# Preparation of a GNN kernel as one block: degree gathers beside the edge rows, normalising on ScalarE, the node table stored inside

## The reference

```python
deg = segment_sum(ones_like(d), d, num_nodes)         # d: edge targets and self loops
dinv = where(deg > 0, rsqrt(deg), 0.0)
norm = dinv[s] * dinv[d]
h = layernorm(x) @ W1                                 # 256 -> 128
out = segment_sum(h[s] * norm[:, None], d) + b1
```

## Time and profile before

| | us |
|---|---|
| median of three runs | 4687.03 |
| profiled execution, its own time | 4687.02 |
| its span, first to last instruction | 4685.2 |
| PE busy | 2944.8 |
| DVE busy | 2124.8 |
| POOL busy | 2607.7 |
| ACT busy | 769.9 |
| preparation (to the first gather of the convolution) | 182.47 |
| its three parts end near | 71.4, 166, 182 |

### The profile page before, as it was taken

The page is one execution under the profiler, slowest core; times in us unless marked ns, Lnnn a source line. Parts: engine busy times, 40 slices in busy tenths (PEclk is TensorE's granted clock), DMA queues, the critical chain, the costliest instruction groups (busy, mean ns, idle before and its releaser), DMA issues. The chain is left out here.

```text
span 4685.2 us, 48041 instructions
## 1 busy us (share of the span) xinstructions
PE 2944.8 (63%) x13048; PEld 2229.0 (48%) x13048; DVE 2124.8 (45%) x3783; ACT 769.9 (16%) x1807; POOL 2607.7 (56%) x2735
## 2 busy tenths in 40 slices
PE   2444444444344444444538989967888777867998
PEld 1333333333233333333437744446666666646665
DVE  7522222222422222222645344447777777864344
ACT  1200000000000000000324422223333333314222
POOL 3577777777477777776350042137777777742000
PEclk9766555556655555566659999978888888875999
DMA  3422222222222222221323355444444444430000
GB/s 93 91 53 53 53 53 53 53 53 53 56 53 53 53 53 53 53 53 45 103 92 118 108 173 197 170 156 139 139 139 138 135 139 138 140 120 21 16 16 24
DMA packets 200949, 409.95 MB, mean 87 GB/s; under 512 B 51843, under 2 KB 125203, under 8 KB 193780
## 3 DMA queue, kind: packets, MB, share of 16 engines
q0 software_dynamic: 102144, 246.72, 19.4%
q1 hardware_dynamic: 91252, 156.35, 9.6%
q10 hardware_dynamic: 7296, 3.70, 0.6%
HBM read 305.82 MB, written 104.44 MB: 88 GB/s over the span
## 5 line engine op out<-in xcount | busy, mean ns | idle before, releaser
L654 POOL DMA_INDIRECT ring<-t_gcn,idx x1568 | 1492.0, 952 | 564.8 <-issue 477.3
L682 PE MATMUL psum<-ring,big 128*128 x3328 | 754.5, 418 | 1095.9 <-DMA ring<-t_gcn,idx 1095.9
L682 PEld LDWEIGHTS psum<-ring,big 128*128 128x128 f32 x3328 | 702.2, 321 | 1242.4 <-issue 1242.4
L1521 POOL DMA_INDIRECT xs_ring<-t_msg,idx x832 | 798.9, 960 | 380.4 <-issue 253.1
L703 DVE TENSOR_TENSOR big<-big,psum 128x1024 f32 x208 | 254.0, 1221 | 1523.0 <-PE psum L682 1522.3
L1644 PE MATMUL psum<-xs_ring,a_hot 128*128 128x264 f32 x1456 | 406.8, 439 | 0.0
L1644 PEld LDWEIGHTS psum<-xs_ring,a_hot 128*128 128x128 f32 x1456 | 330.1, 227 | 74.7
L847 ACT ACTIVATE m_xa<-big,dinv 128x128 f32<-128x128 f32 x49 | 19.5, 401 | 2066.4 <-PEq L641 2066.4
L1409 PE MATMUL psum<-big,a_xnt 128*128 128x512 f32 x784 | 355.2, 596 | 0.5 <-ACT a_xnt L1381 0.5
L1314 POOL DMA_INDIRECT a_back<-t_y,m_addr x98 | 98.0, 1000 | 438.8 <-POOLq L1118 279.8
L430 DVE TENSOR_TENSOR big<-dloc,psum 128x1024 f32<-128x1024 f32 x208 | 252.3, 1214 | 11.3 <-PEq L609 7.2
(11 more groups left out here) (402 smaller groups left out, 4254.0 us busy)
## 6 DMA issues: line engine op xcount, KB each, us to landing
t_msg<-a_rows SPq DMA_DIRECT2D x49, 1056.0 KB, 3.9
a_near<-t_near SPq DMA_DIRECT2D x52, 512.0 KB, 4.3
ring<-t_gcn,idx POOLq DMA_INDIRECT x1568, 2.5
m_xin<-t_tok SPq DMA_DIRECT2D x105, 128.0 KB, 2.1
t_y<-m_yb SPq DMA_DIRECT2D x105, 128.0 KB, 2.0
xs_ring<-t_msg,idx POOLq DMA_INDIRECT x832
xs_ring<-in_x SPq DMA_DIRECT2D x7, 896.0 KB, 11.2
t_gcn<-big SPq DMA_DIRECT2D x14, 448.0 KB, 3.3
```

Source lines behind the costliest of these rows:

```text
L654: g.indirect_dma_start(out=ring[:, p % HALF_RING * 8 + j, :], out_offset=None, in_=t_gcn[conv], in_offset=bass.IndirectOffsetOnAxis(ap=idx ...
L682: m = t.matmul(sums(q)[:, to[j], :], hot[q % 2][:, j, :], ring[:, at[j], :], start=False, stop=j == 7, skip_group_check=True)
L1521: g.indirect_dma_start(out=ring[:, slot, :, :].rearrange("p h c -> p (h c)"), out_offset=None, in_=t_msg, in_offset=bass.IndirectOffsetOnA ...
```

## The change

All of the preparation becomes one block.

- DVE begins with `begin(0)` and `count(0)` ahead of `kcmp`. The other six groups follow behind `ti`, before the row statistics. `began` is now four buffers of one compare (896 columns) each; PE sums each compare as it comes (`tiles_begun`, order of the loops turned, a zero matmul ahead) and DVE waits for a buffer by `s_counted`.
- POOL gathers the seven node-row blocks of group 0, then the 21 edge-row blocks, then the other 42 node-row blocks.
- x is loaded ahead of `idx1` and without waiting for it, with one semaphore for each piece.
- The statistics are finished in the same block. ACT normalises with one `activation` (Identity, scale `rstd`, bias `-mean*rstd`, both a column of SBUF) in place of DVE; ACT still copies the transposes; DVE copies the projected tiles.
- The edge tables are built inside the loop over node tiles: `tables(k)` ahead of tile 7k on DVE, `turn_tables(k)` ahead of `turn(7k)` on PE, `keep_tables(k)` behind tile 7k+2 on ACT.
- The compare and sum of the gathered rows run in seven pieces of seven tiles, behind the slot arithmetic. Degree, square root, reciprocal, scaling and the stores to `t_gcn[0]` follow in the same block.
- `kcmp` lies in `big`, and `nodes`, `first_i` and others use tables that are written later.

The core of the diff (the moved instructions themselves are those of before):

```diff
+                    last_rows(0)
                     g.wait_ge(s_c.sem, s_c.base + 4)
                     for c in range(SCH):
...
+                    for p in range(1, NG):
+                        last_rows(p)
...
+                    def begin(p):
+
+                        for f in range(FT):
+                            i = p * FT + f
+                            if i >= 4:
+                                v.wait_ge(s_counted.sem, s_counted.base + i - 3)
+                            v.tensor_scalar(began[i % 4][:], nodes, first[:, f:f + 1], None, ALU.is_ge).then_inc(s_a.sem, 1)
...
+                    for p in range(1, NG):
+                        begin(p)
+                        if p >= 2:
+                            count(p - 1)
+                    count(NG - 1)
+
+                    for g in range(NG):
+                        v.wait_ge(s_got[g].sem, s_got[g].base + 16)
+                        for n in range(g * GT, (g + 1) * GT):
+                            v.bn_stats(bn6[:, n, :], xs[:, n, :]).then_inc(c.sem, c.up())
...
+                    for n in range(NT + 2):
+                        if n < NT and n % GT == 0:
+                            tables(n // GT)
+                        if n >= 2:
+                            m = n - 2
+                            v.wait_ge(s_f.sem, s_f.base + m + 1)
+                            v.tensor_copy(acc[:, m, :], ps[4 + m % 4][:, 0:HID]).then_inc(s_e.sem, 1)
...
+                    for p in range(NG):
+                        w = slice(p * GT, (p + 1) * GT)
+                        found = began[p % 4][:].rearrange("p (n e) -> p n e", e=P)
+                        v.wait_ge(s_rows[p].sem, s_rows[p].base + 16 * GT)
+                        v.tensor_tensor(found, rows[:, w, :], nid[:, w].unsqueeze(2).to_broadcast([P, GT, P]), ALU.is_le).then_inc(c.sem, c.up())
+                        v.wait_ge(c.sem, c.value())
+                        v.tensor_reduce(below[:, 1, p * GT + 1:p * GT + 1 + GT], found, AX, ALU.add).then_inc(c.sem, c.up())
...
+                    def turn(n):
+                        t.wait_ge(s_used.sem, s_used.base + n + 1)
+                        if n >= 2:
+                            t.wait_ge(s_added.sem, s_added.base + n - 1)
...
+                    def project(n):
+                        t.wait_ge(s_added.sem, s_added.base + n + 1)
+                        if n >= 4:
+                            t.wait_ge(s_e.sem, s_e.base + n - 3)
...
+                    for n in range(NT + 2):
+                        if n < NT and n % GT == 0:
+                            turn_tables(n // GT)
+                        if n < NT:
+                            turn(n)
+                        if n >= 2:
+                            project(n - 2)
...
+                    for n in range(NT + 1):
+                        if n < NT:
+                            if n >= 4:
+                                a.wait_ge(s_hot.sem, s_hot.base + n - 3)
+                            a.activation(xn[n % 4], xs[:, n, :], ACT.Identity, bias=lntmp[:, n:n + 1],
+                                         scale=rstd[:, n:n + 1]).then_inc(s_used.sem, 1)
+                        if n >= 1:
+                            m = n - 1
+                            a.wait_ge(s_hot.sem, s_hot.base + m + 1)
+                            if m >= 4:
+                                a.wait_ge(s_f.sem, s_f.base + m - 3)
+                            a.copy(xnt[m % 4], ps[m % 2][:, 0:D]).then_inc(s_added.sem, 1)
+                        if n % GT == 2:
+                            keep_tables(n // GT)
```

More of the change, by code:

```diff
@@ L210, in gnn_ffn_kernel, with build_hot @@
         firsts_i = sb("firsts_i", [P, -(-ETP // P)], I32, gcn_rows)
[L212 to L216, removed]
+        def build_hot(v, buf, start, ramp, n=8):
+            return v.tensor_tensor(buf, dloc[:, bass.ds(start, n)].unsqueeze(2).to_broadcast([P, n, P]),
+                                   ramp.unsqueeze(1).to_broadcast([P, n, P]), ALU.is_equal)
@@ L229, in gnn_ffn_kernel @@
[L229 to L237, removed]
@@ new lines, in count, with tables @@
+                    def count(p):
+                        w = slice(p * GT + 1, p * GT + 1 + GT)
+                        v.wait_ge(s_counted.sem, s_counted.base + p * FT + FT)
+                        v.tensor_scalar(below[:, 0, w], ps[4 + p % 2][:, 0:GT], -1.0, 0.0, ALU.add, ALU.max).then_inc(s_tile.sem, 1)
+                        v.wait_ge(s_tile.sem, s_tile.base + 2 * p + 1)
+                        v.tensor_copy(tile_of[:, p * GT:(p + 1) * GT], below[:, 0, w]).then_inc(s_tile.sem, 1)
+                    def tables(k):
@@ L353, in _, with tiles_begun, turn_tables @@
                 def _(t):
[L354 to L357 removed]
+                    def tiles_begun(p):
+                        t.matmul(ps[4 + p % 2][:, 0:GT], zeros_b[0:1, :], zeros_b[0:1, 0:GT], start=True, stop=False, skip_group_check=True)
+                        for f in range(FT):
+                            i = p * FT + f
+                            t.wait_ge(s_a.sem, s_a.base + i + 1)
+                            for j in range(GT):
+                                m = t.matmul(ps[4 + p % 2][:, j:j + 1], began[i % 4][:, j * P:(j + 1) * P], ones_b[:],
+                                             start=False, stop=f == FT - 1, skip_group_check=True)
+                            m.then_inc(s_counted.sem, 1)
+                    def turn_tables(k):
                         t.wait_ge(s_d.sem, s_d.base + k + 1)
@@ L378, in _ @@
[L378 to L384 removed]
+                            a.copy(o[:, w], ps[2][0:1, (m + 2) * P:(m + 3) * P]).then_inc(s_b.sem, 1)
+                        a.copy(slot[:, w], ps[3][0:1, 2 * P:3 * P]).then_inc(s_b.sem, 1)
@@ L385, in gnn_ffn_kernel @@
+                    a.wait_ge(s_deg.sem, s_deg.base + 3)
+                    a.activation(deg[:], deg[:], ACT.Sqrt).then_inc(s_deg.sem, 1)
+            s_ld[0].after(16)
             s_ld[2].after(16)
-            s_ld[0].after(16)
-            s_ld[1].after(16 * NG)
+            s_ld[3].after(16)
+            s_in.after(64)
+            s_pool.after(6)
             s_c.after(4)
+            s_dve.after(vector_steps[1])
+            s_a.after(NG * FT)
+            s_stage.after(1 + NG)
+            s_counted.after(NG * FT)
@@ L638, in gnn_ffn_kernel @@
+            for g in range(NG):
+                s_got[g].after(16)
+                s_rows[g].after(16 * GT)
+            s_norm.after(3)
+            s_deg.after(4)
+            for k in (s_used, s_hot, s_added, s_f, s_e):
+                k.after(NT)
             for conv in range(2):
```

454 lines of the change are left out of this document (176 added, 278 removed).

## The result

The kernel after took 4693.45 us, the median of 20 runs (4689.35 to 4697.09), where the kernel before took 4686.02 (4682.91 to 4688.88, 20 runs). The ratio is 1.0017, with a 95% interval of 1.0010 to 1.0023: slower by 7.4 us, and inside the 0.2% that the prediction took for no change. The profiled execution took 4691.6 us with a span of 4689.5; that of before 4687.02 and 4685.2.

The account below looks back on a forecast made before the run. It took the DVE queue and its waits to bound the preparation; its terms put the first ring gather at 189.0 us against 182.5, 6.5 later, giving 4693.5 us, with a range of 4680 to 4718.

Parts of the forecast that it names:

- part 1: DVE queue up to the tile numbers of the edge rows, with the first group's counting added: `ti` at 26.9 us.
- part 2: Counting begun tiles on DVE: six groups at 5.2 us, 31.2, and 0.4 for the last count.
- part 3: Row statistics on DVE: wait for x gone, 16.3 us of `bn_stats` and 2.5 of chain; node tiles start at 77.3.
- part 4: Node tiles and edge tables in one loop: PE and ACT stall behind each table, period 10.1 us, 73.5 in all.
- part 5: From the loop to the first ring gather: memsets and slots 4.7 us, compares 15.4, then 18.1; gather at 189.0.
- both bounds on that pitch: ACT's normalise in the tile loop: at best 0.28 us to the next (4685), at worst 0.61 (4697).
- Rival B: Tile loop: tables hidden beside tile work, ACT alone sets the pace, loop 52 us, kernel 4672; chance 0.12.
- Rival A: Tile loop: PE falls to its low clock in each pause, period 13.7 us, loop 97, kernel 4717; chance 0.17.
- Rival C: Row gathers: compares hold GpSimd up, node-row gathers not early; free below 46 us of delay; no chance of its own.

Follow-up runs that it names:

- e2: The kernel after with PE transposing each edge table behind tile 7k+3 and ACT keeping it behind tile 7k+5: 4668.66 us.
- e3: The kernel after with DVE normalising again and ACT copying the projected tiles again, the tables left in the loop: 4660.16 us.
- the fill: The kernel after with 22 unused PE transposes ahead of each table's transposes but the first: 4686.84 us.
- e1_tables_apart: The kernel after with all seven edge tables ahead of the tile loop on DVE, PE and ACT: 4684.0 us.
- e0_again: The kernel after, unchanged, run again on a slower chip: tile loop 75.3 us, 112.8 us from loop start to ring gather.

## Why the prediction held, step by step

The predicted 4693.5 us is the measured median to 0.1 us, which is better than its steps were, and partly luck: the sum gave a shift of 6.5 us and started from 4687.03, 1.0 above the median of 20 runs; the measured shift is 7.4. Against the profiled run the sum was 2.3 us too late at the ring gather, and errors stand against each other.

| step | predicted | measured |
| --- | --- | --- |
| part 1, `ti` out | 26.9 | 26.3 |
| part 2, counting | 31.6 | 30.0 |
| part 3, statistics and chain | 16.3 + 2.5 | 16.1 + 2.3 |
| loop starts | 77.3 | 74.8 |
| part 4, the loop | 73.5 | 74.4 |
| part 5, memsets and slots; compares; to the ring | 4.7; 15.4; 18.1 | 4.5; 14.9; 18.05 |
| first ring gather | 189.0 | 186.7 |

**Parts 1 to 3** were 2.5 us too long. Most is in counting: 5.2 us for a `begin` with `count` was read off one row pair and taken six times; in the block the six rounds cost 4.7 to 5.0. The wait for x is gone, as said. DVE is busy for 29.45 of the 30.1 us, so nothing else hides there.

**Part 4**, the step that decides, was right in its mechanism and, in sum, in its size. The predicted period was 10.1; with the clock up it was 9.93. The pauses of PE ahead of a table were 2.79, 2.63 and 2.55 (predicted 2.7). ACT's normalise took 0.60 with the next instruction 0.50 behind, as the row at line 1950 had it, so both bounds on that pitch fell away. The last group with its drain took 11.2 (11). That the loop came within 0.9 us has some luck in it too: six periods at 9.93 are 0.9 less than the predicted 60.5, PE's low level at the start cost 1.25 in the first round and not 2, and the falls of the clock, which the sum put at nothing, cost 2.4. e2 and e3 then showed the cause by removing it: with the order of PE's and ACT's queues changed, the period falls to 7.17, with DVE's work put ahead of the tiles to 6.36. Rival B was a wrong forecast of this kernel and the right one for its neighbour: 4672 was its price, with a loop of 52; e2 measured 4668.66, with one of 54.5.

**Rival A** was half right, and this is where a step failed. The prediction held that PE keeps its clock over a pause of 2.7 us, since in the convolution PE stopped at 280.8 and was granted 1.00 until 283.8. One microsecond each, of after:

```profile
99.00:100.00 1.00, 0.00 (x0) 0.00 (x0) 0.92 (x4) 0.00 (x0) 0.69 (x2) 1.00 0.12 37
100.00:101.00 1.00, 0.93 (x9) 0.84 (x10) 0.00 (x0) 0.00 (x0) 0.77 (x1) 1.00 0.25 66
101.00:102.00 1.00, 1.00 (x9) 1.00 (x8) 0.11 (x1) 0.69 (x2) 0.92 (x1) 0.72 0.21 66
102.00:103.00 1.00, 1.00 (x7) 1.00 (x6) 0.18 (x1) 0.86 (x5) 0.69 (x2) 0.50 0.19 61
...
105.00:106.00 1.00, 1.00 (x12) 1.00 (x10) 0.29 (x1) 1.00 (x4) 0.77 (x1) 1.00 0.24 66
```

PE stopped at 97.44 and resumed at 100.07. It was granted full speed through the pause and for about 1.4 us of work more (the 0.72 is a mean of the two levels); then the clock fell to 0.50 (the level of 1.2 GHz) for some 3.5 us, in the middle of dense work. A row that reads 1.00 at the end of a pause does not show that the pause was free; the prediction took "not yet fallen" for "does not fall". The trace of before had a second sign against it, which the prediction did not use. In the same convolution PE stopped at 270.69, and the clock had fallen before 274:

```profile
273.00:274.00 1.00, 0.00 (x0) 0.00 (x0) 0.00 (x0) 0.00 (x0) 0.70 (x2) 0.64 0.13 37
```

A mean of 0.64 between 1.00 and 0.50 puts the fall at about 273.3, 2.6 us after the stop: no longer than the pause of 2.7 that the prediction called safe.

The price stayed small, 2.4 us of the loop and not the 23.5 of rival A, because the clock came back within some 3.5 us (in the first fall 7) and in half of the rounds did not fall. The Trainium skill, page "TensorE: Matmul & The Clock Gate", section "HAM oscillation — how this bites in real kernels", describes a loop that waits some 3 to 5 us for data behind each burst of matmuls and starts every burst at the slow clock. The convolution of before agrees, with its pauses of 5.4 to 5.9 us between 270 and 320 us. The loop of after has shorter pauses, 2.55 to 2.79 us, and the clock fell in two or three of the six rounds that begin behind tiles.

So the early start (2.5 us) and the clock (2.4 to about 7 us) roughly cancel. Of the 7.4 us between the medians, the profiled runs show 4.3; the one of after lies 1.9 below its median, that of before 1.0 above its own. The executions differ in how many rounds fall to the low level, which fits the rest, but no run shows it, and the 6.6 us of the fill's medians stay unplaced.

**Part 5** was right: the compares found all rows there, 14.9 us for seven pairs. **Rival C** had no price, as said: the row gathers ended at about 105.8 (106), 48 us before the first compare.

## What to carry to other kernels

When work is moved into a loop, list for each engine what stands behind it in that queue and does not need it; a table of 2.3 us made a round of 9.9 us here, and one of 7.2 once its consumer stood three to four tiles later. Put a slow step on the engine, and at the place, that runs ahead of the pipeline (normalising) and not on the one at its end (copying results). When no engine is full in a window and the waits form a circle, count the round by hand along the circle, and distrust a share of busy time. A row that shows the clock still up at the end of one pause does not price that pause.

## What the runs showed of the hardware

The clock of TensorE may fall late: after a pause of 2.63 us it stayed at 1.00 for about 1.4 us of resumed work and only then went to 0.50 (rows above). In the round before, with a pause of 2.79, it fell within the pause, about 2.1 us after PE had stopped (0.89 in the microsecond from 87.00, 0.50 from 88.00 on). After four more pauses, each of 2.55 us, it fell once:

```profile
110.27 0.33 PE L499 MATMUL psum<-ident,rowf 128*128 128x128 f32 x1 [2.55 <-DVEq L358]
...
120.47 0.33 PE L499 MATMUL psum<-ident,rowf 128*128 128x128 f32 x1 [2.55 <-DVEq L358]
```
```profile
112.00:113.00 1.00, 1.00 (x7) 1.00 (x6) 0.29 (x1) 0.89 (x4) 0.00 (x0) 0.50 0.00 0
...
121.00:124.00 3.00, 2.52 (x23) 2.23 (x20) 0.88 (x3) 2.21 (x10) 0.00 (x0) 1.00 0.00 0
```

Both rounds are of after, with the same work and the same pause; the first fell to 0.50, the second did not. What decides between them, the runs don't show.

The clock column also reads 1.00 where the matmuls show the low level, as the earlier trace rows did. In e1_tables_apart, window of ten microseconds, then the first transposes of tiles:

```profile
96.30:106.30 10.00, 7.20 (x31) 5.85 (x32) 0.74 (x3) 6.53 (x19) 7.30 (x8) 1.00 0.55 122
```
```profile
104.62 0.63 PE L510 MATMUL psum<-ident,big 128*128 128x128 f32 x2
105.90 0.63 PE L510 MATMUL psum<-ident,big 128*128 128x128 f32 x2
106.95 0.38 PE L510 MATMUL psum<-ident,big 128*128 128x128 f32 x2
107.62 0.38 PE L510 MATMUL psum<-ident,big 128*128 128x128 f32 x2
```

Tiles stand 1.28 us apart and then 0.67, under a clock of 1.00 in both. Before the first change that a trace records, the distance of equal matmuls tells the level, not the column. It also means that PE had been at the low level through all seven tables of e1, whose transposes kept it busy for 10.4 of 21.5 us.

On the two slower chips the same programs took 22 to 23% longer, before as well as after. In the preparation it shows first on DVE, in the compares that count begun tiles (L325): they wait for a releaser that the trace names `remote`, none of the core's own engines or queues, and that neither the trace of before nor that of after has. The row is of the waits of e0_again in 0 to 200 us:

```profile
DVE began L325 <- remote: 19.0, 6, 5.7
```

What holds them is open, and no run was made for it; the tile loops of the kernel after agree within 1 us on all three chips.
